# attention_0: value products and output projection in one PSUM bank, transposes in two, another order of the work in a block

## What is computed

```
q = rope(layernorm(x) @ Wq + bq) * SCALE        # 32 query heads of 64
k, v = the same of Wk and Wv                    # 8 key/value heads, rope on k alone
scores = einsum('buqh,bkuh->buqk', q, k)        # plus a window mask of 128
probs  = softmax(concat([scores, sink]))        # the sink's column is dropped afterwards
out    = einsum('buqk,bkuh->bquh', probs, v)
x      = x + einsum('bquh,uhm->bqm', out, Wo) + bo
```

## Time and profile before

| what | value |
| --- | --- |
| median of 3 runs | 1137.29 us (1137.09 to 1137.39) |
| the profiled execution's own time | 1135.79 us |
| its span, first to last instruction | 1134.0 us |
| PE busy | 1014.3 us, 89% of the span |
| PEld, DVE, ACT, POOL busy | 821.8, 748.9, 628.8, 402.7 us |
| mean granted TensorE clock | 0.959 |
| attention_0's blocks, by their scores | 32.4 us to 346 us of the span, some 28% of it |

### The profile page before, as it was taken

How to read it: one execution, slowest core, us unless ns; L and a number is a source line. 1 busy time by engine, 2 the same in 40 slices (tenths; PEclk the granted TensorE clock), 3 DMA queues, 4 the chain that set the end, 5 groups by cost and what they waited for, 6 DMA issues and landing times. The chain is left out here.

```text
span 1134.0 us, 21031 instructions
## 1 busy us (share of the span) xinstructions
PE 1014.3 (89%) x7004; PEld 821.8 (72%) x7004; DVE 748.9 (66%) x2168; ACT 628.8 (55%) x1557; POOL 402.7 (36%) x381
## 2 busy tenths in 40 slices
PE   5799999999997984889998589999999997879978
PEld 4567777777764553778887368888888885767868
DVE  6667777777654576355655757777777775557984
ACT  2167777777773771233432557777777764334323
POOL 6466666666643012000000544443434331110150
PEclk9999999999999997799999699999999998988999
DMA  4250222111005000254441000001101000000111
GB/s 151 70 179 19 57 48 57 38 30 39 2 1 213 1 2 1 59 122 113 100 115 37 5 29 27 26 28 32 37 14 37 24 10 1 1 1 29 44 40 52
DMA packets 27242, 53.62 MB, mean 47 GB/s; under 512 B 4546, under 2 KB 11778, under 8 KB 26782
## 3 DMA queue, kind: packets, MB, share of 16 engines
q1 hardware_dynamic: 27166, 52.65, 16.9%
HBM read 42.56 MB, written 1.69 MB: 39 GB/s over the span
## 5 line engine op out<-in xcount | busy, mean ns | idle before, releaser
L387 POOL TENSOR_TENSOR sb_a_P<-sb_a_P,sb_a_rec 128x512 f32<-128x512 f32 x128 | 130.2, 1040 | 109.0 <-DVE sb_a_rec L592 109.0
L469 ACT ACTIVATE sb_a_P<-sb_a_nS,sb_a_nm 128x257 f32<-128x257 f32 x256 | 128.2, 508 | 19.7 <-DVE sb_a_nm L581 19.4
L581 DVE CUSTOM_DVE_ANT_0 sb_a_nS<-a_pS,sb_a_mask,sb_a_nsink 128x256 f32<-128x256 f32 x256 | 107.7, 480 | 42.1 <-PE a_pS L705 42.1
L478 ACT COPY sb_xn<-a_pT 128x512 f32<-128x512 f32 x128 | 74.9, 585 | 85.3 <-PE a_pT L719 84.6
L1785 ACT ACTIVATE sb_a_t<-a_pp,sb_a_w 64x512 f32<-64x512 f32 x128 | 87.4, 683 | 21.5 <-PE a_pp L142 17.1
L142 PE MATMUL a_pp<-sb_x_high,sb_a_w_low 128*128 128x512 f32 x188 | 83.4, 444 | 7.9 <-DVE sb_a_P L536 2.5
L719 PE MATMUL a_pT<-sb_ident,sb_a_P 128*128 128x128 f32 x512 | 82.0, 283 | 4.1 <-ACT sb_xn L478 4.1
L142 PE MATMUL a_pY<-sb_a_wo_high,sb_a_OT_low 128*128 128x256 f32 x256 | 74.7, 292 | 11.5 <-DVE sb_a_OT_low L135 9.4
L1858 DVE SCALAR_TENSOR_TENSOR sb_a_t<-a_pp,sb_a_w,sb_a_cs 128x512 f32<-128x512 f32 x64 | 47.8, 748 | 55.6 <-ACT sb_a_t L1785 55.5
L719 PEld LDWEIGHTS a_pT<-sb_ident,sb_a_P 128*128 128x128 f32 x512 | 55.3, 141 | 39.6 <-issue 32.4
L1716 POOL TENSOR_TENSOR sb_a_qT<-sb_a_t 128x512 f32<-128x512 f32 x32 | 41.1, 1286 | 117.4 <-DVE sb_a_t L1861 117.4
(11 more groups left out here) (374 smaller groups left out, 3056.7 us busy)
## 6 DMA issues: line engine op xcount, KB each, us to landing
sb_m_cw<-m_table SPq DMA_DIRECT2D x15, 512.0 KB
sb_a_kr<-sb_a_kall SPq DMA_DIRECT2D x56, 128.0 KB, 2.4
sb_f_w<-f_w SPq DMA_DIRECT2D x12, 384.0 KB, 3.1
sb_m_gu<-m_gu SPq DMA_DIRECT2D x17, 256.0 KB, 6.5
sb_a_w<-a_w SPq DMA_DIRECT2D x16, 257.0 KB, 2.7
sb_m_dn<-m_dn SPq DMA_DIRECT2D x17, 128.0 KB, 6.6
sb_a_w<-a_w SPq DMA_DIRECT2D x8, 259.0 KB, 2.6
sb_a_wo<-a_wo SPq DMA_DIRECT2D x8, 256.0 KB, 2.9
```

Source lines behind the costliest of these rows:

```text
L387: nc.gpsimd.tensor_tensor(part, part, rec[b % 2][:, h, :].rearrange("p (q o) -> p q o", o=1) .to_broadcast([P, 2, S]), ALU.mult).then_inc( ...
L469: out = nc.scalar.activation(Pm[b % 2][:, h, qt, 0:S + 1], nS[:, h, qt, 0:S + 1], ACT.Exp, bias=nm[b % 2][:, h, qt:qt + 1], scale=-1.0, ac ...
L478: nc.scalar.copy(PT[h], pT[:, :]).then_inc(PT_ready, 1)
L581: out = nc.vector.tensor_tensor_reduce(nS[:, h, qt, 0:S], pS[h][:, qt * S:(qt + 1) * S], wmask[:, qt, :], -1.0, nsink[par][:, h:h + 1], AL ...
```

## The change

The bank pO is given to the transposes, which get two banks and use them in turn (head h in bank h % 2), and the values' product and the projection share one bank, pOY. PE's order in a block becomes S, W(0), W(1) of block i-2, T(0), T(1) of i-1, C, O of i-2, T(2), T(3) of i-1. The projection's lag falls from three blocks to two. ACT and DVE follow: ACT copies heads 2 and 3 of block i-2 at the head of its block, then exps(0), `high_OT`, copies 0 and 1, and the other three exps. DVE's `low_OT` moves ahead of the last head's maxima. `weigh(0)` now waits for `added` of the block before, and `project_out` only for `OT_ready`. What runs after the last block follows the same order. No instruction is added or taken away.

```diff
-        pT, pO, pY, pp = (k.ps(ctx, "a0_" + n) for n in ("pT", "pO", "pY", "pp"))
-        v_bank = [pT, pO]
+        pT = [k.ps(ctx, f"a0_pT{i}") for i in range(2)]
+        pOY, pp = (k.ps(ctx, "a0_" + n) for n in ("pOY", "pp"))
+        v_bank = pT
...
@@ scalar, body @@
                     if some(G, b, 2):
-                        evac_PT(*lagged(G, b, 2), 3)
+                        for h in (2, 3):
+                            evac_PT(*lagged(G, b, 2), h)
...
-                    if some(G, b, 1):
-                        evac_PT(*lagged(G, b, 1), 0)
                     exps(G, b, 0)
                     if some(G, b, 2):
                         high_OT(*lagged(G, b, 2))
                     if some(G, b, 1):
-                        evac_PT(*lagged(G, b, 1), 1)
-                    exps(G, b, 1)
-                    exps(G, b, 2)
-                    if some(G, b, 1):
-                        evac_PT(*lagged(G, b, 1), 2)
-                    exps(G, b, 3)
+                        for h in (0, 1):
+                            evac_PT(*lagged(G, b, 1), h)
+                    for h in (1, 2, 3):
+                        exps(G, b, h)
...
@@ vector, body @@
                     for h in range(A0_R):
+                        if h == A0_R - 1 and some(G, b, 2):
+                            low_OT(*lagged(G, b, 2))
                         maxima(G, par, b, h)
-                    if some(G, b, 2):
-                        low_OT(*lagged(G, b, 2))
...
-                    if some(G, b, 3):
-                        add_y(*lagged(G, b, 3))
+                    if some(G, b, 2):
+                        add_y(*lagged(G, b, 2))
...
@@ tensor, turn_P, weigh, project_out @@
-                if not (G == 0 and b == 0 and h == 0):
-                    pe.wait_ge(PT_ready, I)
+                if not (G == 0 and b == 0 and h < 2):
+                    pe.wait_ge(PT_ready, I - 1)
...
                 if p == 0 and some(G, b, 1):
-                    pe.wait_ge(OT_ready, G * NB + b)
+                    pe.wait_ge(added, G * NB + b)
...
-                    if some(G, b, 1):
-                        pe.wait_ge(added, G * NB + b)
...
@@ tensor, body @@
-                    if turn:
-                        turn_P(*lagged(G, b, 1), 0)
-                    if early:
-                        weigh(*lagged(G, b, 2), 1)
-                    if turn:
-                        turn_P(*lagged(G, b, 1), 1)
+                    if out:
+                        for p in range(2):
+                            weigh(*lagged(G, b, 2), p)
+                    if turn:
+                        for h in (0, 1):
+                            turn_P(*lagged(G, b, 1), h)
...
-                        g3, b3 = lagged(G, b, 3)
+                        g2, b2 = lagged(G, b, 2)
...
                     if turn:
-                        turn_P(*lagged(G, b, 1), 2)
-                        weigh(*lagged(G, b, 1), 0)
-                        turn_P(*lagged(G, b, 1), 3)
+                        for h in (2, 3):
+                            turn_P(*lagged(G, b, 1), h)
@@ tensor, after the last block @@
+            for p in range(2):
+                weigh(G, NB - 2, p)
+            for h in (0, 1):
+                turn_P(G, NB - 1, h)
             for qt in range(2):
                 project_out(G, 1, NB - 2, qt)
+            for h in (2, 3):
+                turn_P(G, NB - 1, h)
+            for p in range(2):
+                weigh(G, NB - 1, p)
             for qt in range(2):
                 project_out(G, 1, NB - 1, qt)
```

More of the change, by code:

```diff
@@ L304, in bank_of @@
         def bank_of(n):
-            return pp if n % 2 == 0 or n >= 12 else pY
+            return pp if n % 2 == 0 or n >= 12 else pOY
         EARLY = [("k", 0, 0), ("k", 0, 1), ("q", 0, 0), ("q", 0, 1), ("k", 0, 2), ("k", 0, 3), ("q", 0, 2), ("q", 0, 3)]
@@ L477, in evac_PT @@
                     act.wait_ge(weighed, G * (2 * NB) + (2 * b - 2 + h // 2 + 1))
-                nc.scalar.copy(PT[h], pT[:, :]).then_inc(PT_ready, 1)
+                nc.scalar.copy(PT[h], pT[h % 2][:, :]).then_inc(PT_ready, 1)
             def high_OT(G, b):
@@ L483, in high_OT @@
                     act.wait_ge(projected, G * NB + (b - 1))
-                high_of(nc, OT[b % 2][0][:, :], pO[:, :]).then_inc(OT_high, 1)
+                high_of(nc, OT[b % 2][0][:, :], pOY[:, :]).then_inc(OT_high, 1)
             def body(G, par, last=False):
@@ L509, in _ @@
                 body(G, G % 2, last=(G == A0_G - 1))
-            evac_PT(A0_G - 1, NB - 2, 3)
-            evac_PT(A0_G - 1, NB - 1, 0)
+            for h in (2, 3):
+                evac_PT(A0_G - 1, NB - 2, h)
             high_OT(A0_G - 1, NB - 2)
-            for h in range(1, A0_R):
+            for h in range(A0_R):
                 evac_PT(A0_G - 1, NB - 1, h)
@@ L595, in low_OT @@
                 dve.wait_ge(OT_high, G * NB + (b + 1))
-                low_of(nc, OT[b % 2][1][:, :], pO[:, :], OT[b % 2][0][:, :]).then_inc(OT_ready, 1)
+                low_of(nc, OT[b % 2][1][:, :], pOY[:, :], OT[b % 2][0][:, :]).then_inc(OT_ready, 1)
             def add_y(G, b):
@@ L603, in add_y @@
                     dve.wait_ge(added, G * NB + b)
-                nc.vector.tensor_tensor(k.x[:, 2 * b:2 * b + 2, :], pY[:, :].rearrange("p (c n) -> p c n", c=2),
+                nc.vector.tensor_tensor(k.x[:, 2 * b:2 * b + 2, :], pOY[:, :].rearrange("p (c n) -> p c n", c=2),
                                         k.x[:, 2 * b:2 * b + 2, :], ALU.add).then_inc(added, 1)
@@ L643, in _ @@
                 body(G, G % 2, first=(G == 0), last=(G == A0_G - 1))
[L644 to L648, removed]
+            for b in (NB - 2, NB - 1):
+                low_OT(A0_G - 1, b)
+                add_y(A0_G - 1, b)
             dve.wait_ge(added, A0_G * NB)
@@ L714, in turn_P @@
                 pe.wait_ge(normed, I + 1)
-                if not (G == 0 and b == 0 and h == 0):
-                    pe.wait_ge(PT_ready, I)
+                if not (G == 0 and b == 0 and h < 2):
+                    pe.wait_ge(PT_ready, I - 1)
                 for c in range(2):
                     for qt in range(2):
-                        out = nc.tensor.transpose(pT[:, (2 * c + qt) * P:(2 * c + qt + 1) * P],
+                        out = nc.tensor.transpose(pT[h % 2][:, (2 * c + qt) * P:(2 * c + qt + 1) * P],
                                                   Pm[b % 2][:, h, qt, c * P:(c + 1) * P], k.tile["ident"][:, :])
@@ L725, in weigh @@
                 if p == 0 and some(G, b, 1):
-                    pe.wait_ge(OT_ready, G * NB + b)
+                    pe.wait_ge(added, G * NB + b)
                 for c in range(2):
                     for h in range(2):
-                        out = nc.tensor.matmul(pO[h * A0_D:(h + 1) * A0_D, p * S:(p + 1) * S], values_at(G, 2 * b + c),
+                        out = nc.tensor.matmul(pOY[h * A0_D:(h + 1) * A0_D, p * S:(p + 1) * S], values_at(G, 2 * b + c),
                                                PT[2 * p + h][:, c * S:(c + 1) * S], start=(c == 0), stop=(c == 1))
@@ L737, in project_out @@
                     pe.wait_ge(OT_ready, G * NB + (b + 1))
-                    if some(G, b, 1):
-                        pe.wait_ge(added, G * NB + b)
                 for p in range(2):
-                    out = split_product(nc, pY[:, qt * D:(qt + 1) * D],
+                    out = split_product(nc, pOY[:, qt * D:(qt + 1) * D],
                                         [g[:, p * S + qt * P:p * S + (qt + 1) * P] for g in OT[b % 2]],
@@ L756, in body @@
                         pe.wait_ge(v_ready, NT)
-                    turn, early, out = some(G, b, 1), some(G, b, 2), some(G, b, 3)
+                    turn, out = some(G, b, 1), some(G, b, 2)
+                    if out:
+                        for p in range(2):
+                            weigh(*lagged(G, b, 2), p)
                     if turn:
-                        turn_P(*lagged(G, b, 1), 0)
-                    if early:
-                        weigh(*lagged(G, b, 2), 1)
-                    if turn:
-                        turn_P(*lagged(G, b, 1), 1)
+                        for h in (0, 1):
+                            turn_P(*lagged(G, b, 1), h)
                     if not last:
@@ L771, in body @@
                     if out:
-                        g3, b3 = lagged(G, b, 3)
+                        g2, b2 = lagged(G, b, 2)
                         for qt in range(2):
-                            project_out(g3, par if b == 3 else 1 - par, b3, qt)
+                            project_out(g2, par if b >= 2 else 1 - par, b2, qt)
                     if turn:
-                        turn_P(*lagged(G, b, 1), 2)
-                        weigh(*lagged(G, b, 1), 0)
-                        turn_P(*lagged(G, b, 1), 3)
+                        for h in (2, 3):
+                            turn_P(*lagged(G, b, 1), h)
             for n, (kind, s, c) in enumerate(EARLY):
@@ L786, in _ @@
             G = A0_G - 1
```

(9 more changed lines are left out.)

## The result

The changed kernel takes 1121.53 us (median of 4 runs, 1116.38 to 1121.97); the kernel before takes 1137.19 beside it (4 runs, 1136.42 to 1137.39). The ratio is 0.985, with a 95% interval of 0.983 to 0.987.

What follows compares the result with a forecast made beforehand. PE, busy without a gap, bounds the kernel. Gains of 8.6 (steady blocks), 0.4 (first blocks), 0.3 (start-up), 0.85 (last group) and -0.4 (end) make 9.7 us: execution 1126.1, median 1127.6 us, range 1123.5 to 1133.

Steps and rivals of the forecast that it cites:

- Steady blocks: PE in ordinary blocks: three fewer changes of shape at 0.15 us each, so 8.55 us against 9.00, 0.45 less.
- S to W: PE's change from scores straight into the values' product, seen in no row: taken as 0.15 us, bounds nothing and 0.30.
- The cover of 0.7 us for O: In steady blocks `low_OT` reaches PE at 5.4 us, O is due at 6.15: no stall; W's copies have 0.85.
- First blocks: In a group's first block O stalls 0.35 us for `low_OT`, 0.39 lost in all, leaving a gain of 0.06.
- Added waits: The prediction's step on new waits: O needs its own block's W, W wants four copies; no stall in steady blocks.
- The ends: Start-up and the stage's last part: 0.3 us gained at start-up, 0.85 in the last group, 0.4 lost after the last scores.
- The 2 us put aside for the clock: Later stretches may meet lower granted clocks differently once work moves by 10 us: 2 us either way.
- the offset of one execution (1.5): The median of the runs was taken to lie 1.5 us above the profiled execution, 1127.6 against 1126.1.
- (d): Rival: the 0.15 belongs to semaphore waits on a product's first instruction; blocks stay at 9.00, about 1137.3 us; chance 0.07.
- (c): Rival: copies for W or OT for O come 0.1 to 0.4 us late every block; 1130 to 1134.5; chance 0.13.
- (e): Rival: `high_OT` queues on ACT behind two copies and an exps; blocks 0.85 us longer, 1158 us; chance 0.05.
- (b): Rival: no stall in first blocks, 2.3 us more gained, or S-W is cheaper; 1124 to 1125.4 us; chance 0.13.

Runs made afterwards that it cites:

- split: The changed kernel with the values' product W split again, order S, W(0), T(0), W(1), T(1), two more changes of shape: 1132.17 us, ratio 0.994 to the kernel before.
- low_early: The changed kernel with `low_OT` before the third head's maxima, not the fourth's, in a group's first block: 1120.31 us, and 1118.39 us when run again.
- four_copies: The changed kernel, but the first half of W also waits for all four copies of its block: 1124.48 us, ratio 0.987 to the kernel before.

## Why the prediction was wrong in size

**Steady blocks: right.** 0.15 for a change of shape, three fewer, 8.55: met to 0.01, and split shows that the price is the shape's. S to W, the term that no row showed, was placed at one drain and cost one. The cover of 0.7 us for O and the longer one for W's copies held: no steady block waits. (The prediction counts eight changes of product in the old block; there are nine, with C to O. The six of shape are right, and nothing else hangs on it.)

**First blocks: right in place, a little dear.** Forecast 8.94, measured 8.87: `low_OT` came at 5.62 as said, but PE started 0.06 us after its end, not the 0.15 taken from the earlier trace rows. An idle PE is not the difference, as these rows from the changed kernel's last group show:

```profile
311.58 0.69 DVE L135 TENSOR_TENSOR sb_a_OT_low<-a_pOY,sb_a_OT_high 128x512 fp32r<-128x512 f32 x1
312.42 0.36 PE L142 MATMUL a_pOY<-sb_a_wo_high,sb_a_OT_low 128*128 128x256 f32 x1 [0.54 <-DVE sb_a_OT_low L135]
...
332.12 0.69 DVE L135 TENSOR_TENSOR sb_a_OT_low<-a_pOY,sb_a_OT_high 128x512 fp32r<-128x512 f32 x1 [2.75 <-ACT sb_a_OT_high L130]
```

The first `low_OT` ends at 312.27 and O starts 0.15 later. The second ends at 332.81, and the last O starts 0.05 later, at 332.86, although PE had idled longer there (1.40 against 0.54). What differs in the code is the number of semaphores for which O waits: two at 312.42 (a block b = 0 also has `wo_split`) and in the earlier trace rows (`OT_ready` and `added`), one elsewhere. In seven traces with this order and two banks for T, every O that waits for `low_OT` falls so (0.05 to 0.06, or 0.15); no run was made for it alone. The change itself took the wait for `added` from O, and the prediction kept the old price. The 0.07 us in each of six first blocks, and 0.1 in the last group, are about the 0.4 us by which the middle of the table was missed. low_early shows that the place of `low_OT` on DVE is the cause of the stall, split that its length hangs on when POOL runs.

**The ends: the step that failed.** In "Added waits" I wrote that W wants four copies, and carried it into "The ends": the last but one W there "waits for copies until 9.6". `weigh(p)` waits for 2p + 2 copies, so its first half needs two that are long made, and starts at 322.84 - 314.90 = 7.94, not 9.6. It runs in the time in which ACT makes the others; its 0.86 us (4 steps of 0.216) are won at each place where PE has to wait for copies: once in start-up, twice at the end. The end was forecast at 0.4 lost and gained 1.5, start-up at 0.3 gained and gained 1.3. four_copies turns this back and gives 2.5 of the 2.9 us; the other 0.4 was not followed.

**The clock and the median.** The 2 us put aside for the clock were more than spent: 0.8 us after the attention and 1.8 between profiled execution and median, of which it isn't shown how much is the clock. The kernel before alone had medians of 1137.19, 1140.04 and 1138.32 in three sets of runs, although the first three runs lay within 0.3 us. I took this narrow band for the spread of the time, and the offset of one execution (1.5) as fixed; it was part of the spread. With the ends right the sum for the attention would have been 9.7 + 2.9 = 12.6 (13.0 measured), the forecast 1124.7 and the range, built as it was, 1120.6 to 1130.1, which holds the 1121.53. So the wrong threshold of W is what left the time outside the range. Most of the rest of the 6.1 us by which the forecast missed is the 2.6 that differ from execution to execution or lie after the attention.

**The rivals.** (d) fell with split, (c) and (e) with the blocks of 8.55. (b) did not come about by itself, S to W having its full price, but low_early shows that its first half was to be had for one line. The time lies below (b)'s too: no rival had the ends in it.

## What to carry to other kernels

Where PE is busy without a gap, look inside its busy time: from the last start of one shape to the first of the next against the step of a stream. Products of one shape belong side by side, and in this kernel a second bank for the producer that would otherwise wait for its copy made such an order possible. When costing a wait, read its threshold in the code instruction by instruction: a product in halves waits in halves, and at the ends of a pipeline, where nothing covers it, that was 2.5 us of the 2.9 missed. Judge edits of 1 to 3 us by stretches between two fixed starts in the trace whose clock is granted in full, which here repeat to 0.1 us, and not by totals that spread over 8.

## What the runs showed of the hardware

- From the last start of S, W or T to the first start of another shape: 0.09 to 0.10 us more than a step (S to W in the changed kernel 0.32, where S steps by 0.23), and 0.05 to 0.06 more until the second. C to O and O to T, all of 128 x 128, keep the step (0.23 and 0.12 us), although O and T wait for semaphores; from the last T (f32) to the second C (fp32r) it takes 0.34, one step of each (0.11 and 0.23).
- The totals of one program, unaltered, varied by 8 us in 10 runs (1134.06 to 1141.99) on one core. In two traces of it the stretch from the fourth block's scores to the last projection repeated to 0.04 us; a stretch of 25.80 us before it became 27.59 with the clock at 0.88 in place of 1.00, and one of 24.67 behind it 27.88 with 0.81 in place of 0.93. What decides where these stretches fall, and how much of the 780.3 to 787.3 us after the attention they explain, was not settled.
- In first blocks DVE's copy of two columns (128x2 f32) took 0.53 and 0.55 us (120.79, 122.05) and ended within 0.03 us of the end of POOL's instruction beside it; with POOL idle it took 0.15.
- PE started O 0.05 to 0.06 us after DVE's `low_OT` ended where O waits for one semaphore (332.86, with PE idle for 1.4 us; 124.06, with PE just through with C), and 0.15 after where it waits for two (312.42; 345.95 before). That the second wait is the cause was not tested.
